# Expert layers in tiles of 256 rows, with the weights as the loaded side

## The reference, cut to what matters

```
raw = jnp.einsum('bnd,de->bne', x, w_gating)          # 6 experts
probs = jax.nn.softmax(raw, axis=-1)
gate1 = jnp.max(probs, axis=-1)
idx1 = jnp.argmax(probs, axis=-1)
...
gate1 = gate1 / denom                                  # gate1 + gate2 + EPS
...
expert_in = jnp.einsum('bnd,bnec->ebcd', x, dispatch)  # each row at its first expert only
xn = _layernorm(expert_in, gamma)
hidden = jax.nn.gelu(jnp.einsum('ebcd,edh->ebch', xn, w1), approximate=False)
expert_out = jnp.einsum('ebch,ehd->ebcd', hidden, w2)
out = jnp.einsum('ebcd,bnec->bnd', expert_out, combine)
```

## Time and profile before

| | |
|---|---|
| median of three runs | 865.62 us (864.81 to 866.65) |
| profiled execution | 866.4 us, span 864.6 us |
| PE busy / PEld busy | 607.7 us (70%) / 469.2 us (54%) |
| DVE, ACT, POOL busy | 631.5, 517.7, 324.6 us |
| granted clock of PE, mean | 0.839 of full speed |
| DMA | 56.48 MB, mean 65 GB/s |

### The profile page before, as it was taken

The page is one execution under the profiler, slowest core; times in us unless marked ns, Lnnn a source line. Parts: engine busy times, 40 slices in busy tenths (PEclk is TensorE's granted clock), DMA queues, the critical chain, the costliest instruction groups (busy, mean ns, idle before and its releaser), DMA issues.

```text
span 864.6 us, 11012 instructions
## 1 busy us (share of the span) xinstructions
PE 607.7 (70%) x3076; PEld 469.2 (54%) x3077; DVE 631.5 (73%) x1351; ACT 517.7 (60%) x781; POOL 324.6 (38%) x345
## 2 busy tenths in 40 slices
PE   6994743561826538297653798356999999999987
PEld 4552743561825538274432688323766766666665
DVE  1785597999999999997874111258789888887752
ACT  1587999989889898952322233153565465464432
POOL 0463110222413133141575144305446456465432
PEclk9995876877868677699655799766899999999999
DMA  5380044434455443435111356210000000000000
GB/s 174 121 294 17 0 78 75 82 71 82 83 101 106 85 82 70 78 61 172 58 27 57 100 167 176 79 38 0 2 1 10 0 10 10 1 9 10 1 10 17
DMA packets 26272, 56.48 MB, mean 65 GB/s; under 512 B 4007, under 2 KB 15376, under 8 KB 26005
## 3 DMA queue, kind: packets, MB, share of 16 engines
q0 software_dynamic: 5728, 24.56, 15.1%
q1 hardware_dynamic: 19924, 30.88, 11.7%
q10 hardware_dynamic: 576, 0.52, 0.2%
HBM read 29.89 MB, written 10.17 MB: 46 GB/s over the span
## 4 chain that ended last, share of the span: by engine, by line
PE 44%; DVE 17%; issue 12%; ACT 12%; DMA 7%; POOL 6%; POOLq 1%; SPq 0%; ACTq 0%; DVEq 0%
PE psum L1918 10%; PE psum L1667 3%; DMA s_R<-in_w 3%; PE psum L1731 3%; PE psum L1732 3%; PE psum L1733 3%; PE psum L1851 2%; PE psum L1948 2%; PE psum L1910 2%; DVE s_R L1594 2%; DVE s_R L1200 2%; DVE s_R L1187 2%; POOL s_mean L656 2%; POOL s_part L652 2%; PE psum L1971 2%
## 5 line engine op out<-in xcount | busy, mean ns | idle before, releaser
L1731 PE MATMUL psum<-s_xn_lo,s_split_hi 128*128 128x368 f32 x256 | 95.4, 372 | 138.7 <-ACT s_R L889 134.3
L1731 PEld LDWEIGHTS psum<-s_xn_lo,s_split_hi 128*128 128x128 f32 x256 | 55.1, 215 | 143.5 <-ACT s_R L889 137.1
L1918 PE MATMUL psum<-s_R 128*128 128x368 f32 (+1 forms) x288 | 101.2, 477 | 4.1 <-ACT s_R L1011 4.1
L1206 DVE TENSOR_TENSOR_SCAN s_R<-s_R 128x2944 f32<-128x2944 f32 x16 | 100.7, 6292 | 0.8
L1732 PE MATMUL psum<-s_xn_hi,s_split_lo 128*128 128x368 f32 x256 | 92.3, 361 | 0.0
L1733 PE MATMUL psum<-s_xn_hi,s_split_hi 128*128 128x368 f32 x256 | 92.0, 359 | 0.0
L1011 ACT ACTIVATE s_R<-psum,s_cols 128x368 f32<-128x368 f32 x96 | 50.6, 566 | 51.8 <-PE psum L1912 51.8
L720 POOL TENSOR_TENSOR s_R<-s_R 128x368 f32<-128x368 f32 x47 | 45.0, 957 | 74.6 <-DVE s_R L1473 54.9
L750 POOL TENSOR_TENSOR s_R<-s_R 128x368 f32<-128x368 f32 x48 | 46.7, 973 | 56.9 <-DVE s_R L1594 55.4
L1918 PEld LDWEIGHTS psum<-s_R 128*128 128x128 f32 (+1 forms) x288 | 51.2, 189 | 28.6 <-issue 8.2
L896 ACT ACTIVATE s_R<-psum,s_cols 128x736 f32<-128x736 f32 x64 | 55.4, 877 | 15.9 <-PE psum L1733 11.4
(11 more groups left out here) (242 smaller groups left out, 1640.6 us busy)
## 6 DMA issues: line engine op xcount, KB each, us to landing
s_xnfm<-s_R POOLq DMA_DIRECT2D x14, 1472.0 KB, 10.5
s_R<-in_w SPq DMA_DIRECT2D x28, 256.0 KB
s_R<-in_xg SPq DMA_DIRECT2D x7, 744.0 KB, 4.2
x_sorted<-in_x_init SPq DMA_DIRECT2D x1, 5082.0 KB
s_wBC<-in_wBC SPq DMA_DIRECT2D x8, 256.0 KB, 2.7
s_R<-x_sorted SPq DMA_DIRECT2D x28, 66.0 KB, 2.4
s_R<-in_w SPq DMA_DIRECT2D x1, 1536.0 KB, 6.5
s_R<-y_rows SPq DMA_DIRECT2D x8, 184.0 KB
```

The costliest lines, as they stand in the source:

```text
L1206: dve.tensor_tensor_scan(bufB[:, u], ra[:, u], bufB[:, u], 0.0, ALU.mult, ALU.add).then_inc(ra_free, 1)
L1731: pe.matmul(bank(c), w_hi[:, s, u, k, :], xn_lo[:, a:b], start=True, stop=False)
L1918: ins = pe.matmul(bank((2, 4)[e % 2]), w, fh[0:kk, e % 3, j], start=(j == 0), stop=(j == FT - 1))
```

## The change

The tile becomes 256 rows, and the worst case is 17 tiles. A tile is two blocks of 128 rows (TB = 2). All six w1 are loaded once, beside w2. For each tile VectorE reads the expert's number into a register and copies its w1 and its w2 (512 elements a partition each) into one of two fixed slots `w1_of` and `w2_of`. Layer 1 streams 256 columns, layer 2 now has w2 as the loaded side and the hidden rows moving, also 256 columns. Its result has rows on columns, so VectorE copies it to `oT`, PE transposes it back in two blocks (`turn`), ScalarE copies that to `ot`, and GpSimd stores it with two indirect DMAs. The loops over tiles are written out instead of looped. The regions of `x_sorted` grow, from 9856 to 11520 rows in all, and so does its initial fill.

The core of the diff:

```diff
-    TS = 128
+    TS = 256
     NTILE = (TOK + NE * (TS - 1)) // TS
-    NTILE += NTILE % 2
...
-        RX = TOK + TS
+        RX = (TOK + 2 * (TS - 1)) // TS * TS
...
-            sp.dma_start(w2, t["w2"]).then_inc(w2_ready, 16)
+            sp.dma_start(w1, t["w1"]).then_inc(w12_ready, 16)
+            sp.dma_start(w2, t["w2"]).then_inc(w12_ready, 16)
...
-            with sp.Fori(1, NTILE // 2) as i:
-                for u in range(2):
-                    load_rows(i * 2 + u, u)
-                    load_w1(i * 2 + u, u)
+            for n in range(NTILE):
+                u = n % 2
+                sp.reg_load(x_at[u], tile_x[0:1, n:n + 1])
+                sp.wait_ge(id_ready, n + 1)
+                sp.dma_start(xt[:, u], x_sorted[bass.ds(sp.snap(x_at[u], min_val=0, max_val=XROWS - TS), TS)]
+                             .rearrange("(a p) d -> p a d", p=D)).then_inc(xt_ready[u], 16)
...
+                for a in range(TB):
+                    pool.indirect_dma_start(y_rows, bass.IndirectOffsetOnAxis(ap=ids[:, n, a:a + 1], axis=0),
+                                            ot[:, n % 2, a], None).then_inc(ot_stored[n % 2], 16)
...
+            def gelu(n):
+                u = n % 2
+                act.wait_ge(o_mm, n + 1)
+                act.wait_ge(h_mm, n + 3)
+                act.activation(hid[:, u].rearrange("p j t -> p (j t)"),
+                               psum[:, 2 + 2 * u:4 + 2 * u, :].rearrange("p b n -> p (b n)"), ACT.Gelu)\
+            def rows_out(n):
+                if n >= 2:
+                    act.wait_ge(ot_stored[n % 2], 16 * TB * (n // 2))
+                act.wait_ge(turned, n + 3)
+                act.activation(ot[:, n % 2].rearrange("p a d -> p (a d)"), psum[:, 7, 0:TS], ACT.Copy)\
...
+            def expert_of(n):
+                dve.reg_load(e_at, tile_e[0:1, n:n + 1])
+                return bass.ds(dve.snap(e_at, min_val=0, max_val=NE - 1), 1)
+
+            def first_weights(n):
+                dve.wait_ge(h_mm, n + 1)
+                dve.tensor_copy(w1_of[:, n % 2], w1[:, expert_of(n)].rearrange("p a h -> p (a h)"))\
+                    .then_inc(w1_of_ready, 1)
+
+            def second_weights(n):
+                dve.wait_ge(o_mm, n + 1)
+                dve.tensor_copy(w2_of[:, n % 2], w2[:, expert_of(n)].rearrange("p a j d -> p (a j d)"))\
+                    .then_inc(w2_of_ready, 1)
+
+            def result_copy(n):
+                dve.wait_ge(o_mm, n + 3)
+                dve.wait_ge(turned, n + 2)
+                dve.tensor_copy(oT, psum[:, 6, 0:TS]).then_inc(oT_ready, 1)
+
+            dve.wait_ge(w12_ready, 2 * 16)
+            for n in range(2):
+                first_weights(n)
+            for n in range(2):
+                second_weights(n)
+            tile_in(0)
+            for n in range(NTILE):
+                if n + 1 < NTILE:
+                    tile_in(n + 1)
+                if n + 2 < NTILE:
+                    first_weights(n + 2)
+                if n >= 1:
+                    result_copy(n - 1)
+                    if n + 1 < NTILE:
+                        if n + 1 >= 2:
+                            second_weights(n + 1)
+            result_copy(NTILE - 1)
...
+            def layer1(n):
+                u = n % 2
+                pe.wait_ge(w1_of_ready, n + 1)
+                pe.wait_ge(xeT_ready, n + 1)
+                pe.wait_ge(hid_ready, n + 1)
                 for j in range(HT):
-                    ins = pe.matmul(psum[:, 2 + u, j * TS:(j + 1) * TS], w1[:, u, j * D:(j + 1) * D], xeT[:, u],
-                                    start=True, stop=True)
+                    ins = pe.matmul(psum[:, 2 + 2 * u + j // TB, j % TB * TS:(j % TB + 1) * TS],
+                                    w1_of[:, u, j * D:(j + 1) * D], xeT[:, u], start=True, stop=True)
...
+            def layer2(n):
+                u = n % 2
+                pe.wait_ge(w2_of_ready, n + 1)
+                pe.wait_ge(hid_ready, n + 3)
+                pe.wait_ge(oT_ready, n + 2)
                 for j in range(HT):
-                    ins = pe.matmul(psum[:, 6 + u, 0:D], hid[:, u, j], w2[:, bass.ds(e, 1), j].rearrange("p a d -> p (a d)"),
+                    ins = pe.matmul(psum[:, 6, 0:TS], w2_of[:, u, j * D:(j + 1) * D], hid[:, u, j],
                                     start=(j == 0), stop=(j == HT - 1))
...
+            def turn(n):
+                pe.wait_ge(oT_ready, n + 3)
+                pe.wait_ge(ot_ready, n + 2)
+                for a in range(TB):
+                    ins = pe.transpose(psum[:, 7, a * D:(a + 1) * D], oT[:, a * D:(a + 1) * D], ident[:, :])
+                ins.then_inc(turned, 1)
...
+            tile_in(0)
+            for n in range(NTILE):
+                layer1(n)
+                if n >= 2:
+                    turn(n - 2)
+                if n + 1 < NTILE:
+                    tile_in(n + 1)
+                if n >= 1:
+                    layer2(n - 1)
+            turn(NTILE - 2)
+            layer2(NTILE - 1)
+            turn(NTILE - 1)
```

More of the change, by code:

```diff
@@ L385, in audio_tower @@
         tile_x = take(NTILE, parts=1).bitcast(mybir.dt.int32)
-        ids = take(NTILE).bitcast(mybir.dt.uint32)
+        ids = take(NTILE, TS // D).bitcast(mybir.dt.uint32)
         tile_e = sb("tile_e", [1, NTILE], mybir.dt.int32)
@@ L390, in audio_tower @@
         tile_ready, slot_ready, id_ready = sem("tile_ready"), sem("slot_ready"), sem("id_ready")
-        w1 = take(2, HID)
+        w1 = take(NE, HID)
         w2 = take(NE, HT, D)
         XN = take(B, XD, parts=LS)
-        xt = take(2, XD)
+        TB = TS // D
+        xt = take(2, TB, XD)
         xeT = take(2, TS)
-        ot = take(2, D)
-        w1_ready = [sem("w1_ready0"), sem("w1_ready1")]
-        w2_ready = sem("w2_ready")
+        ot = take(2, TB, D)
+        w1_of = take(2, HID)
+        w2_of = take(2, HID)
+        oT = take(TS)
+        w12_ready = sem("w12_ready")
+        w1_of_ready, w2_of_ready = sem("w1_of_ready"), sem("w2_of_ready")
+        oT_ready, turned = sem("oT_ready"), sem("turned")
         scat_done = sem("scat_done")
@@ L550, in _ @@
             x_at = [sp.alloc_register("x_at0"), sp.alloc_register("x_at1")]
[L551 to L564, removed]
[L566 to L576 removed]
+            sp.wait_ge(scat_done, 16 * B)
+            for n in range(NTILE):
[4 more added lines that the diff above has]
+                             .rearrange("(a p) d -> p a d", p=D)).then_inc(xt_ready[u], 16)
+            for u in range(2):
+                sp.wait_ge(ot_stored[u], 16 * TB * ((NTILE + 1 - u) // 2))
             for c in range(NCH):
@@ L956, in _ @@
             act.sem_inc(ot_ready, 2)
[L958 to L961, removed]
-                    .then_inc(hid_ready, 1)
[L964 to L981, removed]
+            def gelu(n):
[4 more added lines that the diff above has]
+                               psum[:, 2 + 2 * u:4 + 2 * u, :].rearrange("p b n -> p (b n)"), ACT.Gelu)\
+                    .then_inc(hid_ready, 1)
+            def rows_out(n):
[3 more added lines that the diff above has]
+                act.activation(ot[:, n % 2].rearrange("p a d -> p (a d)"), psum[:, 7, 0:TS], ACT.Copy)\
+                    .then_inc(ot_ready, 1)
+            gelu(0)
+            for n in range(NTILE):
+                if n + 1 < NTILE:
+                    gelu(n + 1)
+                rows_out(n)
             stage_end(act, 4)
@@ L1398, in _ @@
             dve.sem_inc(id_ready, 2)
[L1400 to L1403, removed]
-                dve.tensor_scalar(xeT[:, u], psum[:, u, 0:TS], col("ffn_gamma"), None, ALU.mult).then_inc(xeT_ready, 1)
[L1406 to L1410, removed]
+            dve.sem_inc(oT_ready, 2)
@@ L1843, in expert, with tile_in @@
[L1843 to L1849, removed]
+            def tile_in(n):
+                u = n % 2
+                pe.wait_ge(xt_ready[u], 16 * (n // 2 + 1))
+                for a in range(TB):
+                    ins = pe.transpose(psum[:, u, a * D:(a + 1) * D], xt[:, u, a, 0:D], ident[:, :])
+                ins.then_inc(xT_mm, 1)
@@ L1890, in _ @@
+            for s in (xT_mm, h_mm, o_mm, turned):
+                pe.sem_inc(s, 2)
+            tile_in(0)
+            for n in range(NTILE):
+                layer1(n)
+                if n >= 2:
+                    turn(n - 2)
+                if n + 1 < NTILE:
+                    tile_in(n + 1)
[4 more added lines that the diff above has]
+            turn(NTILE - 1)
             stage_end(pe, 4)
```

52 lines of the change are left out of this document (18 added, 34 removed).

## The result

The changed kernel takes 869.34 us (median of ten runs, 867.47 to 872.67); before, ten runs beside it gave 865.21 (864.03 to 866.65). The ratio is 1.0047, 95% interval 1.0035 to 1.0059: slower by 4.1 us, and the forecast was slower by 5.1.

A forecast was written before the change was run, and what follows sets the result against it. TensorE was taken to bound the expert stage, with one wait on the w1 load. 17 x 3.92 = 66.6 against 14 x 4.65 = 65.1, plus first start, last turn and tail, gave +5.1 us: 870.7, range 866.5 to 879.5.

The forecast's parts named there:

- What bounds: Expert stage: TensorE nearly the limit, its one wait the w1 load, costing 0.77 us in 256 rows.
- Unit price: TensorE's fp32 matmul is two passes; one of 256 columns takes 0.217 us, against 0.110 at 128 columns.
- Step and padding: Expert loop on TensorE: 17 tiles x 3.92 = 66.6 us, against 14 x 4.65 = 65.1 before.
- 16% against 21%: Expert stage: the 16% gain from removing the w1 wait is eaten by 21% more rows from padding.
- Its row of the sum: VectorE's work per expert tile: 3.2 us with both register loads unhidden at 0.60, under TensorE's 3.92.
- the first start: First layer 1 of the expert stage starts at 481.5, before 480.47, from row load, transpose, gamma and weight copies.
- the 0.4 taken for the four weight copies: Before the first layer 1: VectorE's four weight copies add 0 to 0.9 us, taken as 0.4.
- The rival in which VectorE sets the step: Expert loop: unhidden register loads, dear copies and GpSimd waits make VectorE's tile 4.5 us; 879.4 us, chance 0.14.
- Half clock and the first steps: Expert stage start: TensorE at half clock until near 487; layers 1 start at 481.5 and 486.45, layer 2 ends 490.4.
- The last turn and the tail: Expert stage end: new wait of 0.58 before tile 16's layer 2; tail 5.64 us, before 4.83; each adds 0.8.
- Clock pays it back: Rival: half-clock start and 548 to 605 run faster, saving 2.7 and at most 9.3; about 866 us, chance 0.13.

The follow-up runs named there:

- second profile: The changed kernel run once more with no edit against the changed kernel; median 868.95 us, ratio to before 1.0037, expert stage 83.35 us.

## Why the prediction was right, step by step

**What bounds.** Right. The wait on w1 was the only one of weight: the kernel with w1 resident and tiles of 128 rows gains 9.3, with four result slots 10.6 (10.8 in the stage), where 14 x 0.77 = 10.8 was read from the trace. That the last two agree so closely is partly chance, since the pair of tiles also fell to 3.79.

**Unit price.** 0.217 was forecast for a pass of 256 columns, 0.216 measured. The line through 128 and 368 columns held at 256 and at 512. The rule of the Trainium skill (TensorE: Matmul & The Clock Gate, "Back-to-back issue gap") would give 109 ns at 256 columns and 216 ns at 512; the measurement decides: each of the two passes of a fp32 matmul takes twice that, 0.216 and 0.43 us.

**Step and padding.** 3.92 forecast, 3.90 measured, against 4.65; 17 steps against 14. Leaving three tiles out gave 11.3 back. The prediction set 16% against 21%, which have different bases; the products it took, 66.6 against 65.1, are the right comparison.

**VectorE.** Its row of the sum was too high (3.2 against 1.97 a step) because the register load was taken at SyncE's 0.6. It mattered only for the first start, forecast at 481.5 against a landing of 479.72, 1.8 later, and measured 1.38 later (478.88 against 477.50, in the second profile 480.40 against 479.02): the 0.4 taken for the four weight copies was not there, they were done before the transposes were. The rival in which VectorE sets the step is out.

The Trainium skill (SBUF — State Buffer, "SBUF: two separate sides") says that such a copy and GpSimd shut each other out. The trace shows a mild form: in the changed kernel seven row stores that begin within the w2 copy take 1.22 us in place of 0.97, in six other places the copy takes 0.49 or 0.50 in place of 0.43, and nothing waits for it.

```profile
498.20 0.97 POOL L693 DMA_INDIRECT y_rows<-s_R  x1 [1.71 <-ACT s_R L959]
...
499.42 0.43 DVE L1406 COPY s_R<-s_R 128x512 f32 x1
499.47 1.22 POOL L693 DMA_INDIRECT y_rows<-s_R  x1 [0.30 <-issue]
```

**Half clock and the first steps.** Here lies the largest error of the sum. From the landing of the first rows to layer 1 of tile 2 it gave 10.7 us (479.72 to 490.4); the two profiles have 9.7 (477.50 to 487.23) and 10.2 (479.02 to 489.19). VectorE's 0.4 is one part. The other is the gap between the first two layers 1: 1.50 was forecast, 0.91 and 1.12 measured. The sum let the half clock last 7.3 us after the landing, nearly as before; it was over between 482 and 483 in the first profile and between 484 and 485 in the second. Why it rose earlier is not shown. That the second layer 1 came out as forecast (1.97 for 2.00) is luck: 1.3 slow passes were in the sum, in the run all eight were fast, 8 x 0.216 = 1.73, and the other 0.24 stood at the start after the stop, which the sum did not have. The 14 steps to tile 16 then took 54.5 (487.23 to 541.73) in place of 54.9, and from there to the read-back 12.1 in place of 11.9. Together, 1.0 + 0.4 - 0.2, that is the 1.1 between 5.1 and 3.97.

**The last turn and the tail.** As forecast in size. From the timeline of the changed kernel:

```profile
545.44 0.42 DVE L1412 COPY s_R<-psum 128x256 f32<-128x256 f32 x1 [2.69 <-PE psum L1872]
...
545.92 0.44 PE L1880 MATMUL psum<-s_ident,s_R 128*128 128x128 f32 x2 [0.52 <-DVE s_R L1412]
```

TensorE stops 0.52 there (0.58 forecast); from the last result copy at 548.12 to the read-back it is 5.70, forecast 5.59. The sum missed one bound, though. GpSimd starts each of the last two pairs of stores 0.45 after the pair before, and stores back to back are 0.30 apart, so it had only 0.15 us to spare; the profile's own chain even runs through it. A quicker tail on TensorE alone would have gained little before GpSimd set it, as the kernel without the turn showed.

**Clock pays it back.** The stretch from 548 to 605 has a mean clock of 0.67 after and 0.65 before, and the time behind the stage is 307.9 after and 308.0 before; nothing came back there.

## What to carry to other kernels

A fixed worst-case tile count is part of a tile's price: 28 to 17 tiles of twice the size is 21% more rows, so a row has to get 18% cheaper (1 - 28/34) only to break even, and here it got 16% cheaper. When a stage waits for one load and its engine is otherwise full, take the wait away at the same tile size first; here that was worth 9.3 us, and 10.6 with more result slots. Making weights resident beat more slots of the same load, 9.3 against 4.7: the loads shared an in-order list with the row loads, and TensorE then waited for rows. Before taking work off one engine, look how near the next one is: without the turn GpSimd took over the tail. Before widening the moving side, divide the measured passes by their columns at two widths: if both lie on a line through nearly zero, width saves nothing.

## What the runs showed of the hardware

A fp32 matmul runs as two passes of 0.110, 0.216, 0.310 and 0.43 us at 128, 256, 368 and 512 columns at full clock; the line through them starts near zero, so the weight load of 128 columns is hidden even at 128. After 13 us of dense matmuls, the first of them at half clock, and a pause of TensorE of 2.58 us the clock was back at 0.50 before the first layer 1; after 22 us of them and a pause of 2.57 it stayed at 1.00 into that layer and fell to 0.50 behind it. A register load on VectorE between two copies added less than 0.1 us, on SyncE 0.6 between two DMA issues. An indirect row store that usually lands in 2.25 us took 4.21 once in a profiled execution, and with two slots that reached TensorE, for 0.24 us.
